# A fused four-layer kernel: late rows written behind the next head's loads, factors turned one output later, products behind the first output tile, and heads' Newton steps on GpSimd

## Time and profile before

| | before |
|---|---|
| median of 3 runs | 764.28 us (763.38 to 765.21) |
| the profiled execution's own time | 764.83 us |
| its span | 763.0 us |
| PE busy | 653.5 us (86%) |
| DVE busy | 537.2 us (70%) |
| ACT busy | 465.7 us (61%) |
| POOL busy | 183.3 us (24%) |
| mean granted TensorE clock | 0.973 |

### The profile page before, as it was taken

How to read it: one execution, slowest core, us unless ns; L and a number is a source line. 1 busy time by engine, 2 the same in 40 slices (tenths; PEclk the granted TensorE clock), 3 DMA queues, 4 the chain that set the end, 5 groups by cost and what they waited for, 6 DMA issues and landing times.

```text
span 763.0 us, 9361 instructions
## 1 busy us (share of the span) xinstructions
PE 653.5 (86%) x3336; PEld 282.3 (37%) x3370; DVE 537.2 (70%) x1025; ACT 465.7 (61%) x451; POOL 183.3 (24%) x205
## 2 busy tenths in 40 slices
PE   5999899998999979887888588788898787979695
PEld 2577545454464513222222121122232111547263
DVE  5656430505507089996999499999999998777656
ACT  1244333332233389997999599999999988213211
POOL 3721100201403221491146200413700031021001
PEclk9999999999999999998999799999999999999898
DMA  8000200000401601114110511111011121400430
GB/s 308 1 0 2 85 1 0 1 0 1 124 1 32 182 15 52 52 40 138 52 52 27 150 52 52 54 52 52 19 34 52 53 63 50 111 0 15 111 125 28
DMA packets 32238, 42.77 MB, mean 56 GB/s; under 512 B 5184, under 2 KB 19264, under 8 KB 31808
## 3 DMA queue, kind: packets, MB, share of 16 engines
q1 hardware_dynamic: 32192, 42.17, 18.8%
HBM read 31.60 MB, written 10.55 MB: 55 GB/s over the span
## 4 chain that ended last, share of the span: by engine, by line
PE 43%; DVE 24%; ACT 15%; issue 9%; SPq 4%; POOL 3%; DMA 1%; POOLq 0%; DVEq 0%; ACTq 0%
ACT w_hh L974 11%; PE ps L701 7%; DVE hid L1244 6%; DVE hid L1239 6%; PE ps L686 6%; PE ps L729 5%; PE ps L673 4%; PE ps L611 3%; PE ps L738 3%; PE ps L592 3%; SPq L357 2%; PE ps L714 2%; PE ps L487 2%; PE ps L518 2%; DVE st L1050 1%
## 5 line engine op out<-in xcount | busy, mean ns | idle before, releaser
L974 ACT ACTIVATE w_hh<-hid 128x2048 f32<-128x2048 f32 x128 | 247.5, 1934 | 10.7 <-DVE hid L1244 10.3
L611 PE MATMUL ps<-w_hh,v_h 128*32 128x512 f32 x1024 | 139.2, 616 | 31.5 <-ACT w_hh L974 30.3
L592 PE MATMUL ps<-q_s,k_s 64*128 64x512 bf16 x256 | 100.5, 392 | 17.9 <-DVE hid L1239 17.6
L1239 DVE TENSOR_TENSOR hid<-ps,probs 128x1024 f32<-128x1024 f32 x86 | 104.6, 1216 | 12.3 <-PE ps L592 9.5
L1244 DVE SCALAR_TENSOR_TENSOR hid<-ps,probs 128x1024 f32<-128x1024 f32 x86 | 104.6, 1217 | 5.6 <-PE ps L592 4.5
L592 PE MATMUL ps<-q_w,k_w 64*128 64x512 bf16 x256 | 100.5, 392 | 0.8 <-DVE hid L1244 0.7
L946 ACT ACTIVATE probs<-ps 128x1024 f32<-128x1024 f32 x86 | 89.7, 1043 | 5.1 <-PE ps L592 5.0
L592 PE MATMUL ps<-q_g,k_s 128*128 128x512 bf16 x222 | 71.5, 392 | 19.2 <-DMA q_w<-qk_rows 12.2
L1146 DVE SCALAR_TENSOR_TENSOR hid<-ps,s_b,rot 128x512 f32<-128x512 f32 x16 | 11.9, 750 | 91.2 <-ACT rot L915 91.2
L1566 POOL TENSOR_SCALAR rs<-mv 128x4 f32<-128x4 f32 x32 | 7.5, 234 | 278.5 <-DVE mv L1053 278.3
L592 PEld LDWEIGHTS ps<-q_w,k_w 64*128 64x128 bf16 x256 | 23.7, 93 | 109.8 <-DVE hid L1244 57.7
(11 more groups left out here) (263 smaller groups left out, 1005.6 us busy)
## 6 DMA issues: line engine op xcount, KB each, us to landing
qk_rows<-part SPq DMA_DIRECT2D x48, 128.0 KB, 2.3
w_hh<-w_rows SPq DMA_DIRECT2D x4, 1024.0 KB, 9.7
qk_rows<-part_g SPq DMA_DIRECT2D x24, 128.0 KB, 2.3
q_g<-qk_rows SPq DMA_DIRECT2D x32, 96.0 KB, 2.2
k_s<-qk_rows SPq DMA_DIRECT2D x32, 96.0 KB, 2.3
k_w<-qk_rows SPq DMA_DIRECT2D x32, 96.0 KB, 2.5
q_s<-qk_rows SPq DMA_DIRECT2D x32, 96.0 KB, 2.5
q_w<-qk_rows SPq DMA_DIRECT2D x32, 96.0 KB, 2.5
```

The lines of the kernel that those rows point to most:

```text
L592: last = mm(ps[:, base + half, :], k_op[rows, u, keys], q_op[rows, u, half * CHUNK:(half + 1) * CHUNK], start=True, stop=True)
L611: last = mm(ps[VW * g4:VW * g4 + VW, 6, :], v_h[:, u, mt, :], ee[:, mt % 2, g4 * CHUNK:(g4 + 1) * CHUNK], start=(mt == 0), stop=(mt == BT ...
L974: A(ee[:, mt % 2, :], zz[:, mt % 2, :], ACT.Exp).then_inc(S["e"], 1)
L1239: v.tensor_tensor(zz[:, mt % 2, 0:SEQ], banks[:, 2 * CHUNK:4 * CHUNK], gg[s % 3], ALU.add).then_inc(S["z1"], 1)
```

## The change

Four things are changed. The rows of chunk 2 are written after the loads of head 4 have been issued (ahead of those of head 5), and the rows of chunk 3 after those of head 7 (ahead of those of head 8). In stage B the turn of the factors comes after output 2 rather than output 1 of the first square product, and ACT's two copies come one gelu later. `c_prep` comes after the first tile of the way out rather than before it. The three Newton steps for the heads' roots are done by GpSimd at the head of `heads_b`, in four instructions each, and DVE only prepares their start.

```diff
+        def of_heads(t, h0, h1):
+            return t[:, 0:2 * HEADS * CT].rearrange("p (a n) -> p a n", a=2)[:, :, h0 * CT:h1 * CT]
...
-                if n in (4, HEADS - 1):
-                    c = 2 if n == 4 else 3
+                if n in (5, HEADS):
+                    c = 2 if n == 5 else 3
                     sp.wait_ge(S["lo_c"], c + 1)
...
                     last.then_inc(S["m1_b"], 1)
-                    if c >= 2 and o == 1:
+                    if c >= 2 and o == 2:
                         pe.wait_ge(S["fac_c"], c - 1)
...
                 if 1 <= c < CHUNKS - 1:
                     c_prep_turn(c - 1)
-                    c_prep(c - 1)
                 pe.wait_ge(S["yo_b"], c)
                 for k4 in range(CT):
...
-                last.then_inc(S["y_b"], 1)
+                    if k4 == CT - 1:
+                        last.then_inc(S["y_b"], 1)
+                    if 1 <= c < CHUNKS - 1 and k4 == 0:
+                        c_prep(c - 1)
...
-                    if c >= 2 and o == 1:
+                    if c >= 2 and o == 2:
                         c_high(c - 2)
-                    if c >= 2 and o == 2:
+                    if c >= 2 and o == 3:
                         c_middle(c - 2)
...
+            def heads_start(h0, h1):
+                heads_square(h0, h1)
+                dve.sem_inc(S["ms_o"], 1)
...
                     if at == (9, 2):
                         dve.wait_ge(S["to_a"], 2)
-                        heads_square(0, HEADS)
-                    if at in ((9, 3), (9, 4), (9, 5)):
-                        heads_newton(0, HEADS, "ms_o" if mt == 5 else None)
+                        heads_start(0, HEADS)
...
                     if at == (15, 3):
                         dve.wait_ge(S["to_a"], 4)
-                        heads_square(*G1)
-                    if at in ((15, 4), (15, 5), (15, 6)):
-                        heads_newton(*G1, "ms_o" if mt == 6 else None)
+                        heads_start(*G1)
...
             def heads_b(b, h0, h1):
                 pool.wait_ge(S["ms_o"], b + 1)
+                r, half_of, tmp = (of_heads(w, h0, h1) for w in (rstd, nh, nt))
+                for _ in range(3):
+                    me.step(g.tensor_tensor(tmp, r, r, ALU.mult))
+                    me.step(g.tensor_tensor(tmp, tmp, half_of, ALU.mult))
+                    me.step(g.tensor_scalar(tmp, tmp, 1.5, None, ALU.add))
+                    me.step(g.tensor_tensor(r, tmp, r, ALU.mult))
```

More of the change, by code:

```diff
@@ L1036, in whole, with by_heads @@
                 return t[:]
-            def of_heads(h0, h1):
+            def by_heads(h0, h1):
                 def view(t):
-                    return t[:, 0:2 * HEADS * CT].rearrange("p (a n) -> p a n", a=2)[:, :, h0 * CT:h1 * CT]
+                    return of_heads(t, h0, h1)
                 return view
@@ L1304, in heads_square @@
                 me.wait()
-                of = of_heads(h0, h1)
+                of = by_heads(h0, h1)
                 me.step(v.tensor_scalar(of(nv), ms_o[:, :, at], 1.0 / VH, RMS_EPS, ALU.mult, ALU.add))
                 rsqrt_start(of(rstd), of)
+            def heads_start(h0, h1):
+                heads_square(h0, h1)
+                dve.sem_inc(S["ms_o"], 1)
             def heads_newton(h0, h1, done=None):
-                of = of_heads(h0, h1)
+                of = by_heads(h0, h1)
                 rsqrt_newton(of(rstd), of, done)
```

## The result

| | before | after |
|---|---|---|
| median | 763.83 us (763.15 to 765.21, 4 runs) | 741.38 us (740.04 to 743.95, 4 runs) |
| ratio, 95% interval | | 0.9708 (0.9678 to 0.9738) |
| the profiled execution's own time | 764.83 us | 743.95 us |
| its span | 763.0 us | 742.1 us |
| mean granted TensorE clock | 0.973 | 0.982 |

The change gains 22.4 us by the medians, where 24.2 was worked out (forecast 740.1, range 737.0 to 745.5). The profiled execution of after is the slowest of its four, 2.6 us above their median, so its rows sum to 20.9 us and not to 22.4. Executions of one kernel differ with the granted clock: of 25 of the kernel before, seven at 761.7 to 762.7 us show a mean of 0.978 to 0.982, the others, at 763.2 to 765.4, one of 0.970 to 0.977.

A forecast was written before the change was run, and what follows sets the result against it. No engine bounds the whole kernel; ScalarE sets stage C's beat and TensorE bounds stage B. Terms 15.66 + 4.14 + 0.4 + 1.66 + 2.33 = 24.2 us, from the median 764.28 to 740.1 us, range 737.0 to 745.5.

The forecast's parts named there:

- Edit 1: Stage C, late rows written behind the loads: the stalls at heads 3 and 6 go whole, 6.22 + 9.44 = 15.66 us.
- Edit 2: Stage B, factors after output 2: 4.14 us at chunk 2 (2.44 wait, 1.70 low clock), 0.4 us at chunk 3.
- rival 1: Start of stage C: head 0's loads become the wait, TensorE idles over 2 us, low clock follows; 743.8 us, chance 0.10.
- A wait on a load at head 0 of over 2 us: Before head 0's first product: named beforehand as a sign that the forecast is wrong.
- the sign of being right, under 1 us: Before head 0's first product: a wait of under 1 us would show the forecast right.
- Exps over 2.8 us apart in heads 3 to 6: Stage C: named beforehand as a sign that the forecast is wrong.
- Edit 3: Stage B, products behind the first tile of the way out: 0.83 us at chunks 1 and 2 each, 1.66 us.
- Edit 4: Heads 9 and 15, Newton steps on GpSimd: 1.25 and 1.08 us above the beat go, 2.33 us.
- Rivals 2, 3 and 4: Head 8 stall, 749.5 (0.05); VectorE and GpSimd hold-up, 755.4 at most (0.03); stage C low clock, 770 with 50 tiles (0.03).

The follow-up runs named there:

- x4: Changed kernel with chunk 2's rows held back too, so all 36 writes stand between the loads of heads 7 and 8; 742.87 us, ratio 0.9718.
- edit 2 alone: Kernel before with only the factors turned after output 2 instead of output 1 in stage B; 760.07 us, ratio 0.9956.
- x1: Changed kernel with the last chunk's factors turned after output 1 again, ScalarE's two copies back at outputs 1 and 2 there; 741.75 us, ratio 0.9702.
- edit 1 alone: Kernel before with only the late rows written behind the loads of heads 4 and 7; 749.37 us, ratio 0.9813.
- x5: Changed kernel, head 0's plain-row loads issued before the wait for gained rows, last chunk's factors turned inside output 2; 739.24 us, again 738.82 us.

## Why the prediction was right, and where it was off

- **Edit 1, "15.66 us": right.** 6.17 + 9.44 = 15.6 in the trace of after, 14.3 to 14.9 in the times when alone. The writes found room, as placed: chunk 2's end at 347.1 and head 5's loads start at 352.4, 5 us later, which is the slack given. Chunk 3's end at 417.1, and head 8's loads start at 420.5, when they are allowed. Where 13 us to spare were given at heads 4 and 7, and 11 at head 8, the loads landed 11.6, 12.4 and 9.9 us before TensorE took them, and x4 leaves 3.5 of the 9.9. One part of the sum was less certain than it looked: 2.5 us of head 3's 6.22 are the low clock behind its wait, and in the trace of edit 2 alone the same wait comes without it.
- **Edit 2, "Sum 4.14 us" at chunk 2: the wait right, the clock half right.** With it alone chunk 2 is 4.35 us shorter. In the combination only 2.66 of that are edit 2's (from 47.28 us without it to 44.62), since with edit 3 the wait of 2.44 us costs no low clock. I had read a stretch at half clock behind one wait as the wait's consequence. In the sum of all four edits it is still counted once, so the total doesn't suffer; that is luck of the combination and not of the reasoning.
- **Edit 2, "I take 0.4 us" at chunk 3: this step failed.** The piece from chunk 3's way in to the first exp got no shorter in any of five traces with the edit at this chunk. It is 0.03 us longer without edit 3, 0.25 in x4, 0.77 with edit 2 alone, 0.93 and 1.25 in two traces of the changed kernel. The mechanism was the one worked out: loads later, TensorE waits, and x1 confirms it. The size was missed by two things. First the wait, 1.18 to 2.14 us instead of 0.8. Counted from chunk 3's way in, the loads start 1.4 us later (1.6 was given), but TensorE comes 1.5 us earlier rather than 1.27, and the ten loads take 7.05 to 7.81 us from first issue to landing, against 6.89 before. In the four traces of these five that have edit 1 too, one of head 0's ten is issued 0.6 to 1.2 us late; with edit 2 alone they go evenly. Second, I compared the first product, not the first exp. From the one to the other it is 5.77 us before, 6.42 in the profiled execution of after, and 6.0 to 6.6 in the other four, longer where the low-clock stretch that every trace has at the start of stage C begins before the exp. It is 6.37 with edit 1 alone too, where no load was waited for, so this part isn't shown to be the wait's doing. In all it is rival 1, held at 0.10, in a milder form.
- **The signs named beforehand.** "A wait on a load at head 0 of over 2 us" was a sign of being wrong, and it stands in the profiled execution (2.14 us); the sign of being right, under 1 us, stands in no trace with this edit at chunk 3 and the loads unsplit. The forecast time held all the same, since chunk 3's term is small beside the other four. "Exps over 2.8 us apart in heads 3 to 6" was a poor sign: head 4 has steps of 3.03 and 3.53 us after, and had 3.02 and 3.53 before.
- **Edit 3, "1.66 us": right**, 0.89 at each of two chunks, and 1.6 us when taken back. No wait of the sums took its place.
- **Edit 4, "2.33 us": right in size**, 1.0 + 1.6 us up to the last exp, some 2.0 when the 0.37 behind it and the 0.21 at head 11 are taken off, and 2.2 to 2.6 in the times when alone. Behind (9, 3) the tiles are at the beat (10.84 us for four), but the preparation that stays costs 0.2 us more than before, at (9, 2) and at (15, 3). From (15, 4) to (15, 7) the last three exps come closer than the beat (7.37 us instead of 9.19), more than the 1.08 given. GpSimd's twelve steps take 477.69 - 472.77 = 4.9 us, against 5 estimated between 3.3 and 6.5.
- **Rivals 2, 3 and 4** left no trace: no wait at head 8, sums at 1.22 us beside the Newton steps, heads 5 to 8 at the beat (21.64 to 21.85 us) and head 4 at 22.83 as before (22.82).
- **The sum.** The total came out 1.8 us high, 24.2 for 22.4. Chunk 3's term, 0.4 forecast and -0.03 to -1.25 measured, explains 0.4 to 1.65 of it by the traces, and the three small losses above, which the sum had at nothing, another 0.7; edits 3 and 4 were a little larger than given. The rest can't be told from the scatter: four executions of the changed kernel spread over 3.9 us.

## What to carry to other kernels

On a queue that issues in program order, a late producer's writes belong behind the next loads that are already allowed; a wait at the head of such a queue is paid by everybody behind it. Before an operation is put later to hide a wait, follow what hangs on its result to the next stage's first use: at the last round there may be no slack left, and the last round may need a place of its own (here inside the output). And a stretch at the low clock behind a wait is not that wait's price for certain: look at the same wait in several traces first.

## What was unexpected of the hardware

- The same wait of TensorE (2.43 or 2.44 us) is followed by a stretch at the 1.2 GHz level (granted clock 0.5) in three kernels and by the full 2.4 GHz level in two others. The wait for head 4's loads does the same: the low level follows in three traces (waits of 3.35 to 3.41 us), and not in that of edit 2 alone (3.57). Another stretch, at the start of stage C, stands in every trace, also where no load was waited for: with x5 it lasts 6.8 us.
- In every trace one of the twenty loads that follow the stage's last writes takes 0.87 to 1.62 us of SyncE's queue instead of 0.42, not always the same one. In the changed kernel it fell on head 0's loads (256.27, 1.62 us above), with edit 2 alone on head 1's, where it cost nothing.
- VectorE's last split of chunk 3 (two tiles in SBUF in, none in PSUM) takes 2.21 us in the trace of after, beside GpSimd's copy, which takes 2.34 instead of 1.49. Before, VectorE began its split (246.15) ahead of GpSimd's product (L1609, 246.46) and kept its 1.22 us; GpSimd's product took 1.93 us instead of 1.15, so the hold-up was there too and fell on GpSimd. VectorE's sums with one SBUF tile stay at 1.22 us beside GpSimd's Newton steps. The page "SBUF — State Buffer" of the Trainium skill (section "Who interferes with whom") states this contention for a VectorE instruction with two SBUF inputs beside a GpSimd one that reads SBUF, and none for one SBUF input; the traces agree with both halves. Here it cost nothing, since the writes were just as long in the queue: GpSimd ended at 246.94, the queue was free at 247.02.

```profile
242.14 2.21 DVE L1206 TENSOR_TENSOR part<-raw,part 128x1024 bf16<-128x1024 f32 x1 [1.46 <-ACT part L911]
...
243.36 2.34 POOL L1616 TENSOR_SCALAR part_g<-g_q 128x512 bf16<-128x512 f32 x1
```
